# Score stacks and keys of two attention layers on 128 array rows instead of 96

## What is computed

```
x = x + L0_attn(layernorm(x))     # softmax(q k^T / sqrt(8), causal) v, 16 heads of 8, then Wout
x = x + L0_ffn(layernorm(x))      # experts
x = x + L1_attn(layernorm(x))     # 16 query heads of 8 with rotary positions, one k and one v head
x = x + L1_ffn(layernorm(x))      # fp4 gate, up, down
```

## Time and profile before

| | |
|---|---|
| median of 3 runs | 732.33 us (731.49 to 733.81) |
| the profiled execution's own time | 732.03 us |
| its span, first to last instruction | 729.9 us (2.1 us of its time lie outside) |
| granted TensorE clock, mean over the span | 0.909 |
| TensorE matmuls busy | 593.2 us, 81% |
| VectorE busy | 489.1 us, 67% |
| ScalarE busy | 332.4 us, 46% |
| GpSimd busy | 213.6 us, 29% |

### The profile page before, as it was taken

How to read it: one execution, slowest core, us unless ns; L and a number is a source line. 1 busy time by engine, 2 the same in 40 slices (tenths; PEclk the granted TensorE clock), 3 DMA queues, 4 the chain that set the end, 5 groups by cost and what they waited for, 6 DMA issues and landing times.

```text
span 729.9 us, 12641 instructions
## 1 busy us (share of the span) xinstructions
PE 593.2 (81%) x4398; PEld 394.5 (54%) x4398; DVE 489.1 (67%) x1184; ACT 332.4 (46%) x638; POOL 213.6 (29%) x216
## 2 busy tenths in 40 slices
PE   1468999998789658979889698689799999997574
PEld 0334556665454325869776465345455666545453
DVE  7588787776684635765363565866866788466993
ACT  1110576774455634435443233155456666664221
POOL 5331010102032242262164213452022001334764
PEclk9995799999898979999998799589999999999876
DMA  7517686559311112122131311312102110000001
GB/s 244 131 25 175 139 231 120 112 142 200 69 38 55 29 49 73 52 62 67 52 91 34 91 34 63 85 54 67 46 25 68 48 47 19 19 14 0 15 15 29
DMA packets 50589, 53.41 MB, mean 73 GB/s; under 512 B 6271, under 2 KB 43377, under 8 KB 50497
## 3 DMA queue, kind: packets, MB, share of 16 engines
q1 hardware_dynamic: 48481, 48.42, 26.0%
q0 software_dynamic: 2048, 4.20, 2.1%
HBM read 33.56 MB, written 21.10 MB: 75 GB/s over the span
## 4 chain that ended last, share of the span: by engine, by line
PE 38%; DVE 17%; ACT 3%; issue 3%; POOL 2%; DMA 0%; POOLq 0%; SPq 0%; DVEq 0%; ACTq 0%
PE ps L597 6%; PE ps L1206 5%; PE ps L581 4%; PE ps L557 4%; DVE mx L793 3%; PE ps L1194 2%; PE ps L623 2%; ACT pT L680 2%; PE ps L560 1%; PE ps L584 1%; DVE xn L1100 1%; PE ps L1185 1%; PE ps L1188 1%; PE ps L1187 1%; PE ps L1186 1%
## 5 line engine op out<-in xcount | busy, mean ns | idle before, releaser
L793 DVE TENSOR_REDUCE mx<-ps 128x2 f32<-128x1024 f32 (+2 forms) x192 | 196.2, 1040 | 81.4 <-PE ps L560 80.2
L680 ACT ACTIVATE pT<-ps 128x512 f32<-128x512 f32 x320 | 182.7, 596 | 67.8 <-PE ps L584 63.7
L560 PE MATMUL ps<-mask_qk,identb 128*128 128x128 bf16 (+2 forms) x352 | 92.9, 264 | 0.0
L597 PE MATMUL ps<-pT,vA 128*32 128x512 f32 (+3 forms) x1024 | 82.8, 459 | 1.4 <-ACT pT L680 1.4
L584 PE MATMUL ps<-mask_kq,identb 128*128 128x128 bf16 (+1 forms) x320 | 83.7, 262 | 0.0
L557 PE MATMUL ps<-stA 96*128 96x512 bf16 (+3 forms) x256 | 64.9, 336 | 15.3 <-DVE mx L793 12.1
L557 PE MATMUL ps<-kA,stA 96*128 96x512 bf16 (+3 forms) x256 | 62.5, 325 | 16.4 <-DVE mx L793 11.7
L581 PE MATMUL ps<-stB 96*128 96x512 bf16 (+3 forms) x256 | 64.0, 316 | 10.1 <-ACT pT L680 9.1
L581 PE MATMUL ps<-stB,kA 96*128 96x512 bf16 (+3 forms) x256 | 62.8, 311 | 10.4 <-ACT pT L680 9.9
L597 PEld LDWEIGHTS ps<-pT,vA 128*32 128x32 f32 x1024 | 42.3, 114 | 35.1 <-issue 24.5
L1233 ACT ACTIVATE pT<-ps 128x512 f32<-128x512 f32 x46 | 27.4, 595 | 64.1 <-PE ps L1188 64.1
(11 more groups left out here) (293 smaller groups left out, 1119.2 us busy)
## 6 DMA issues: line engine op xcount, KB each, us to landing
stA<-stack_scratch SPq DMA_DIRECT2D x48, 192.0 KB, 3.3
stB<-stack_scratch SPq DMA_DIRECT2D x48, 192.0 KB, 4.6
stack_scratch<-part SPq DMA_DIRECT2D x12, 384.0 KB, 3.2
stack_scratch<-part SPq DMA_DIRECT2D x12, 256.0 KB, 3.3
pairs_scratch<-b1r SPq DMA_DIRECT2D x2, 1472.0 KB
pT<-pairs_scratch SPq DMA_DIRECT2D x46, 64.0 KB, 1.9
outs_scratch<-pT SPq DMA_DIRECT2D x46, 64.0 KB, 1.5
w_lo<-w_scratch SPq DMA_DIRECT2D x8, 256.0 KB, 3.8
```

The source lines that it names most:

```text
L560: last = pe.matmul(diagonal, identb[:], mask_qk[:].unsqueeze(1).broadcast_to([P, per, P]), start=False, stop=True)
L597: last = pe.matmul(ps[VW * j:VW * (j + 1), O_BANK, kb * P:T], vA[:, kb, g * HG + j if layer == 0 else 0, :], pT[:, g % 2, j, off:off + w], ...
L680: act.activation(dst_, src, ACT.Exp, scale=SCALE).then_inc(a["ex"], 1)
L793: nc.vector.tensor_reduce(mx[:, g % 2, qb, heads[0]:heads[0] + nh], src, AX.X, ALU.max).then_inc(a["maxd"], 1)
```

## The change

One constant: the stacks and keys reach over all 128 partitions.

```
--- before.py
+++ after.py
@@ -57,7 +57,7 @@
 TERMS = 6
 SR = TERMS * DK
 MR = SR
-KR = 96
+KR = P
 SCALE = float(DK) ** -0.5
```

## The result

| | before | after |
|---|---|---|
| median, with the prediction | 731.91 us (4 runs, 728.51 to 733.81) | 719.94 us (4 runs, 719.41 to 720.65) |
| ratio, 95% interval | | 0.9842 (0.9804 to 0.988) |
| a second comparison | 731.25 us (17 runs, 727.56 to 733.67) | 722.19 us (6 runs, 717.16 to 725.72) |
| ratio, 95% interval | | 0.9879 (0.9844 to 0.9914) |
| span of the profiled execution | 729.9 us | 718.9 us |

The way was right and the size was not.

A forecast was written before the change was run, and what follows sets the result against it. TensorE was taken to bound the steady attention, with TensorE and VectorE both near their limit in the low-clock stretches. Gains of 2.25 + 0.66 + 0.7 = 3.6 us off 732.03 gave 728.4 us, range 723.2 to 733.8.

The forecast's parts named there:

- What a row costs, and the memsets: Score matmuls and GpSimd memsets: columns and elements per partition set the time, so 0 us added; matmul bound 1 us.
- What is left is the clock: TensorE's low-clock stretches: rows in use, zeros included, weigh in the granted clock; mean from 0.91 to about 0.93 or more.
- The rival by which rows don't weigh: Whole kernel: row counts don't affect the granted clock, nothing moves, 732.0 us. Chance 0.25.
- First, the values' products: Layer 1, line 597 at 503.04 and 543.61 us: neither clock fall comes, 1.19 + 1.06 = 2.25 us go.
- Second, 457 to 463 us: Layer 1's first scores: VectorE's maxima become the bound, only its 0.66 us wait for TensorE goes.
- the rival of more: Both VectorE waits, values' products, 0.66 and some 2.5 us before 481.02 go: about 8.8 us, 723.2 us. Chance 0.15.
- Third, 54 to 82 us: Layer 0's first scores: VectorE's waits of 1.47 and 1.92 us may shrink; bounds 0 and 3.39 us, 0.7 taken.
- what that is worth: The list of gains from a higher clock: values' products 2.25, 457 to 463 us 0.66, 71 to 82 us 0.7; sum 3.6 us.
- The slower rival: Clock rises where VectorE is the bound, then is missing in TensorE's own work: two 1.7 us losses, 735.4 us. Chance 0.1.

The follow-up runs named there:

- the control: Buffers over 128 partitions as in the changed kernel, but score matmuls in both layers use 96 rows: 730.78 us, ratio 1.002 to the kernel before.
- again128: The changed kernel run once more, unaltered, giving its second trace: 722.19 us, ratio 0.9879 to the kernel before.
- s_only: The changed kernel with line 581's turned scores back on 96 rows, line 557 on 128: 723.72 us, ratio 0.9914 to the kernel before.
- st_only: The changed kernel with line 557's scores back on 96 rows, line 581 on 128: 727.1 us, ratio 0.9959 to the kernel before.
- steady96: The changed kernel with three of eight batches, the steady ones, on 96 rows: 719.91 us, ratio 0.9868 to the kernel before.
- ones: The changed kernel with the stacks' added rows holding ones and the keys' zeros, by more memsets: 729.71 us, ratio 0.998.
- dup96: 96 rows everywhere, with 88 matmuls of line 557 issued twice in batch 0 of both layers: 734.0 us, ratio 1.0049 to the kernel before.
- r112: The changed kernel with score matmuls on 112 rows: 723.58 us, ratio 0.9904 to the kernel before.

## Why the prediction was wrong

**What a row costs, and the memsets.** Right: 275 ns for 274, and 6.92 us for 6.92. The half us that goes with the mixed row counts lies within the prediction's bound of 1 us either way.

**What is left is the clock.** Right in its mechanism. The control and the after kernel differ by rows alone, and the clock goes from 0.914 to 0.936 or more. The rival by which rows don't weigh, with the Trainium skill's page "TensorE: Matmul & The Clock Gate", section "Loop structure matters more than you think", on its side, is answered by that: the loop nest was the same, and the clock was not. One row that the prediction leant on was chance in part, though: before, the clock stayed at 0.50 from 71.4 to 81.7 us behind a busy window, and in the control, on 96 rows too, it is up from 67.0 to 77.2 us.

**First, the values' products.** 2.25 forecast, 3.1 measured in both traces. Both falls stayed away, and 29 of line 597's matmuls take 2.27 us on the chain where they took 3.27. What was missing is the rest of those stretches: I had counted line 597 alone and left out the score, mask and turning matmuls ahead of it, from 501.50 to 503.04 us at the lower clock. (The 1.06 also set 29 matmuls against 30; by the same rate it is 1.13.)

The chain of waits of the changed kernel there, beside the earlier trace rows:

```profile
494.45 2.27 PE ps L597 x29
...
533.66 2.21 PE ps L597 x30
```

**Second, 457 to 463 us.** 0.66 forecast, 1.1 measured (0.5 of it in the control too), right in kind: the wait is gone at 455.80, and VectorE's maxima set the pace. But the low stretch also ended sooner (471.8 us, and with starts 7.0 to 7.5 us earlier there that is 479 on the old trace, where it was 481.0), and 1.1 us more went by 484. The control has none of these 1.1. They had stood in the rival of more, and belonged in the forecast.

**Third, 54 to 82 us.** 0.7 forecast, 1.8 and 1.7 measured from 62 us on, 0.5 in the control. The waits of 1.47 and 1.92 us are 0.55 and 1.26. I had gone toward the lower bound because an earlier rise might bring an earlier fall. It did bring one, a low stretch at 75.8 us, and it cost less than it gave.

**What the sum left out.** Layer 0's last values' products, 228 to 235 us, stood at the lower clock as well; the first trace wins 1.3 us there. I had priced two such products in layer 1 and not looked for the third. It is won in five of the eight traces with more rows in layer 0, and in none of those without. The second trace of the changed kernel is one of the exceptions: there the low stretch came earlier, cost 1.1 us by 228 and gave 1.2 back by 246.

The failing step is thus the list behind "what that is worth": one entry missing, three too small, each by a choice toward no gain. With the half us at full clock the parts make 8.8 us in the first trace, of which the control wins 0.8 by chance, and 7.7 in the second, for 3.6 forecast.

**The slower rival** came in part, at the price that the prediction gave it. In the second trace a low stretch lies in TensorE's own work at 195.5 us and costs 1.6 us. It is there in five of the eight traces with more rows in layer 0 (`again128`, `s_only`, `st_only`, `steady96`, `ones`), in `dup96`, and in none of the four others on 96 rows in layer 0. In the second trace and in `ones` 3.0 us more are lost between 270 and 300 us, in `st_only` and `r112` 1.1, and in no trace without more rows in layer 0; whether that is chance stays open. The gains outweigh both, as the 10 executions on 128 rows show. (By the prediction's own words its chance of slower should have been 0.07 and not 0.09.)

**The range** also took one execution's low stretches for the kernel's. The profile before, at 0.909 and 729.9 us, is somewhat on the slow side of the 72 (medians 0.913 and 729.0), and the spread from 725 to 735 us between executions was not visible in three runs.

## What to carry to other kernels

When the granted clock is below 1 in stretches, read it per stretch and list every one of them that holds work on the path, before pricing any; then ask what each engine is bound by at the upper clock, as only the slack up to VectorE's pace can be won. Here a matmul on 96 or 112 rows took as long as one on 128, so rows of zeros were free, and they brought back about a quarter of a us for each us less at the lower clock. A low stretch that goes in one place can come in another, so look for losses in the new traces as well as for gains. Compare several executions' clocks before explaining a difference of under 1% between two profiles: in this kernel chance alone moves it by up to 1.4%.

## What the runs showed that I had not expected

That 64 rows beside 128 cost some 160 us, about 0.1 us at each change, where 96 rows beside 128 cost 2 to 3 ns at each. That the same program's time follows its mean clock so closely (0.26 us per us of low time, correlation 0.94 over 72 executions). And that 32 rows of zeros in 1024 matmuls take some 34 us off the time at the lower clock.
